# Two gated attention and feed-forward layers in one kernel: all phases in one block, routing by quarters inside the first attention, and expert rows in fixed regions

## The chip, the cores and the metric

One core of a Trainium2 chip runs the whole program. The metric is the device time of one execution in microseconds (us); lower is better.

## What is computed

`x` is 32 batches of 128 rows of 128 numbers, in float32. Four sublayers are added to it one after the other, each on the row-normalised `x`, each scaled by the tanh of a gate. Cut to what matters:

```python
# first attention: one head, 77 keys and values per batch from ctx
Q = ln(x) @ Wq + bq;  K = ctx @ Wk + bk;  V = ctx @ Wv + bv
context = softmax(where(mask == 0, -inf, Q @ K.T / sqrt(128))) @ V
x = x + tanh(g_xattn[0]) * (ln(context) * gamma + beta)
# first feed-forward: 8 experts, one per row, and a shared one
idx = argmax(ln(x) @ router.T)
y = (silu(ln(x) @ gate[idx].T) * (ln(x) @ up[idx].T)) @ down[idx].T
ys = silu(ln(x) @ w_gate_s.T) * (ln(x) @ w_up_s.T) @ w_down_s.T
x = x + tanh(g_ffn[0]) * (y + ys)
# second attention: 16 heads of 8, a bias by distance, padding, projection Wo
x = x + tanh(g_xattn[1]) * (attend(ln(x), ctx) @ Wo + bo)
# second feed-forward: 8 maps of 128 x 128, one chosen per row by signature
x = x + tanh(g_ffn[1]) * (ln(x) @ W[t] + b[t]),  t = argmax(ln(x) @ sign(sigs).T)
```

## The kernel before

Every engine has its program written out by hand; engines meet through semaphores. A block is a set of five programs, one per engine, and ends in a barrier of all engines. There are three blocks.

**Setup** (`build`, L282 to L370). SyncE loads `x` in four quarters of 8 batches into `X`. ScalarE issues 18 small loads (`early`); one semaphore counts them all, so everything that needs any of them waits for the last, `cst`. VectorE computes mean and variance of the rows of `x`, GpSimd the inverse root (`pow`). TensorE multiplies the query and key weights of first attention into one matrix `wqk`. Then SyncE copies the bias table into the tensor `wide_qk` (2048 rows of 77) and issues 10 further loads (`late`).

**First attention** (`attend_0`). Work goes by pairs of batches: 16 pairs, numbered 0 to 15. `pipeline` (L105) gives each engine a list of stages with lags; in a turn an engine runs each stage of its list once, for the pair that stands `lag` pairs back. The middle turns are a loop with registers for the pair's number. Per pair: ScalarE normalises x (`norm`, L555, with `nb0` and `rstd0`); TensorE transposes it and projects the context (`project`, L457 to L463: values of both attentions, `M`, keys of second attention, a row `crow`); ScalarE copies `M` and the keys out (L533); `scores` adds `crow` by a matmul of one row; VectorE adds the mask and takes the maximum `nmax` (`masked`, L589); ScalarE exponentiates; TensorE transposes and multiplies by the values into bank U (`weigh`, L488); VectorE takes the statistics of U (`attend_stats`, L608 to L614) and writes `t1` (L618), with which bank U is free again; GpSimd inverts (`inv_std0`); VectorE writes the new x (`residual`, L628) and its statistics; GpSimd makes `r1` and `nb1` (`inv_std1`, L664 to L670, `pow` in L666); ScalarE normalises (`norm1`, L564), GpSimd copies that into `XN` (L674), TensorE transposes it, ScalarE copies it twice (`xn1T` and `XNT`), and TensorE makes the router's logits, which ScalarE stores in `LG` (L548). SyncE loads context, mask and 1/16 of the expert weights per turn, then fills `sorted_x` with blank rows. At the end VectorE scales the weights `wds`, `wdn`, `wo1`, `bo1`, `w2` and `b2` by the gates (L648).

**Third block**: `feed_forward_0`, then `attend_1`, on each engine one behind the other.

- *Routing.* VectorE takes the argmax for all 32 batches at once (L918 to L923). TensorE counts ranks within and across batches (L807, L808), and VectorE makes from them the row in `sorted_x` where each row of x goes: the rows sorted by expert, each expert's part padded to 128 (L927 to L943), and the table `tile_experts` (L946 to L956), which holds the expert of each of the 39 tiles of 128 rows.
- *Scatters.* GpSimd waits for `slot` and issues 32 indirect DMAs, one per batch, from `XN` to `sorted_x` (L775). Column 128 of each row holds where the result shall go.
- *Shared feed-forward* meanwhile, 6 chunks of 4 batches (`hidden`, L792 and L793; silu, L872; product, L910; `down`, L801; addition, L915). The last two chunks' worth is done in second attention.
- *Expert tiles.* SyncE loads tile after tile from `sorted_x` once all scatters have landed (L769), up to four tiles ahead. TensorE transposes, multiplies by `wgu` of the tile's expert (L832; the expert comes from a register load, L824, one per four tiles), ScalarE and VectorE make `hid`, TensorE multiplies by `wdn` (L848), and GpSimd scatters the result to `routed` (L781).
- *Second attention and feed-forward* go by single batches in a pipeline of 25 stages on TensorE. They are not rewritten.

## Time and profile before

| what | us |
|---|---|
| median of 3 runs (616.97 to 621.12) | 618.58 |
| the profiled execution, its own time | 621.03 |
| its span, from the first to the last instruction | 619.2 |
| TensorE busy | 534.1 (86%) |
| VectorE busy | 403.0 (65%) |
| GpSimd busy | 367.2 (59%) |
| ScalarE busy | 343.9 (56%) |

The shares are means over stages with different limits. TensorE's clock has two levels, 1.2 and 2.4 GHz; the granted clock is given as a share of 2.4 GHz. Engines are named PE (TensorE matmul), PEld (its weight load), DVE (VectorE), ACT (ScalarE), POOL (GpSimd) and SP (SyncE); `q` behind a name is that engine's sequencer. L is the line of the kernel before.

### The profile page before, as it was taken

How to read it: one execution, taken by the hardware profiler on the slowest of the kernel's cores; microseconds unless marked ns; L12 is line 12 of the kernel's file. 1: busy time of each engine (PE TensorE's matmuls, PEld its weight loads, DVE VectorE, ACT ScalarE, POOL GpSimd, SP SyncE). 2: the span in 40 equal slices, each digit the busy share in tenths (PEclk: the TensorE clock that was granted, in tenths of full speed). 3: DMA queues.
4: the chain of work that ended last, by engine and by line, in shares of the span. 5: the costliest groups of instructions: out<-in, count | busy, mean ns of one | idle time of the engine just before them, and what ended most of it. 6: DMA issues, size and time to landing. Idle time of an engine off the chain costs nothing.

```text
span 619.2 us, 14247 instructions
## 1 busy us (share of the span) xinstructions
PE 534.1 (86%) x3643; PEld 339.4 (55%) x3643; DVE 403.0 (65%) x1188; ACT 343.9 (56%) x1013; POOL 367.2 (59%) x740
## 2 busy tenths in 40 slices
PE   0189999769626999989999999999999999999963
PEld 0167777536314666666665565656656566565520
DVE  6138888756103434435888888888888888888731
ACT  0137888531002555528767767677676766767510
POOL 4206677626760555543477776777768777776541
PEclk9989999769677999988999999999999999999965
DMA  7822225401111222210000000000000000000000
GB/s 191 128 78 70 76 74 168 103 1 39 52 51 27 78 76 79 63 35 5 10 11 19 10 17 17 8 17 8 17 15 10 17 8 17 11 10 10 10 5 8
DMA packets 39731, 25.50 MB, mean 41 GB/s; under 512 B 9727, under 2 KB 37025, under 8 KB 39698
## 3 DMA queue, kind: packets, MB, share of 16 engines
q1 hardware_dynamic: 34946, 19.58, 12.4%
q0 software_dynamic: 2272, 4.67, 2.4%
q10 hardware_dynamic: 2480, 0.85, 0.6%
q8 instruction: 15, 0.25, 0.2%
q14 instruction: 18, 0.15, 0.1%
HBM read 15.68 MB, written 10.04 MB: 42 GB/s over the span
## 4 chain that ended last, share of the span: by engine, by line
PE 61%; issue 5%; POOL 4%; another core or an unknown queue 3%; DVE 3%; ACT 1%; DMA 1%; POOLq 0%; SPq 0%; DVEq 0%; ACTq 0%
PE bank L1164 12%; PE bank L1112 10%; PE bank L1103 7%; PE bank L1125 7%; PE bank L1099 3%; POOL routed L781 3%; PE bank L832 3%; PE bank L1136 2%; PE bank L1173 2%; PE bank L792 2%; PE bank L793 2%; PE bank L801 1%; PE bank L1152 1%; PE bank L848 1%
## 5 line engine op out<-in xcount | busy, mean ns | idle before, releaser
L1215 ACT ACTIVATE PRT<-bank 77x512 f32<-77x512 f32 x128 | 74.6, 583 | 18.0 <-PE bank L1112 16.0
L1112 PE MATMUL bank<-cst,SC 128*77 128x128 f32 x512 | 81.0, 281 | 0.2 <-ACT SC L1207 0.2
L1164 PE MATMUL bank<-w,xn3T 128*128 128x512 f32 x128 | 75.7, 675 | 2.5 <-DVE XN L1372 2.0
L1207 ACT ACTIVATE SC<-SC,low 128x77 f32<-128x77 f32 x256 | 67.4, 346 | 1.2
L1112 PEld LDWEIGHTS bank<-cst,SC 128*77 128x77 f32 x512 | 59.6, 150 | 14.5 <-issue 13.9
L781 POOL DMA_INDIRECT routed<-ys,to x39 | 37.2, 953 | 45.4 <-issue 25.4
L1304 DVE TENSOR_TENSOR SC<-bank,biasQ 128x616 f32<-128x616 f32 x64 | 51.1, 799 | 15.3 <-PE bank L1103 15.3
L1125 PE MATMUL bank<-PRT,VP 77*32 77x128 f32 x1024 | 54.5, 285 | 0.7 <-ACT PRT L1215 0.7
L1372 DVE TENSOR_TENSOR XN<-bank,OH 128x512 f32<-128x512 f32 x64 | 44.3, 692 | 15.1 <-PE bank L1164 11.8
L1103 PE MATMUL bank<-KB,QT 32*128 32x308 f32 x256 | 51.6, 480 | 0.0
L1311 DVE TENSOR_REDUCE top<-SC 128x8 f32<-128x616 f32 x64 | 50.5, 789 | 1.1
L1438 POOL TENSOR_TENSOR sum<-XN 128x512 f32<-128x512 f32 x32 | 41.2, 1289 | 15.9 <-DVE XN L1372 15.9
L775 POOL DMA_INDIRECT sorted_x<-XN,slot x32 | 30.9, 965 | 24.2 <-DVE slot L943 14.7
L972 DVE TENSOR_TENSOR hid<-actg,bank 128x256 f32<-128x256 f32 x39 | 16.4, 422 | 39.2 <-ACT actg L882 34.7
L832 PE MATMUL bank<-wgu,xsT 128*128 x78 | 40.9, 606 | 0.3 <-ACT xsT L877 0.3
L1417 POOL TENSOR_TENSOR x2b<-x,bo 128x128 f32<-128x128 f32 x32 | 14.5, 453 | 39.9 <-DVE x L1346 39.9
L1440 POOL TENSOR_TENSOR sum<-sum 128x256 f32<-128x256 f32 x32 | 35.7, 1115 | 2.5
L872 ACT ACTIVATE sg<-bank 128x512 f32<-128x512 f32 x12 | 7.1, 597 | 49.9 <-remote 29.6
L1325 DVE TENSOR_TENSOR SC<-SC,top 128x616 f32<-128x616 f32 x32 | 33.8, 1058 | 0.0
L1125 PEld LDWEIGHTS bank<-PRT,VP 77*32 77x32 f32 x1024 | 20.2, 108 | 24.5 <-issue 18.4
L1243 ACT ACTIVATE xn3T<-bank 128x128 f32<-128x128 f32 x32 | 8.9, 277 | 37.5 <-PE bank L1152 37.5
L1164 PEld LDWEIGHTS bank<-w,xn3T 128*128 128x128 f32 x128 | 19.7, 194 | 18.1 <-ACT OHT L1248 6.9
(222 smaller groups left out, 1295.7 us busy)
## 6 DMA issues: line engine op xcount, KB each, us to landing
sorted_x<-blank SPq DMA_DIRECT2D x10, 258.0 KB, 4.0
xs<-sorted_x SPq DMA_DIRECT2D x39, 64.5 KB
X<-in_x SPq DMA_DIRECT2D x4, 512.0 KB, 7.6
wgu<-in_wgu SPq DMA_DIRECT2D x16, 128.0 KB
y<-routed SPq DMA_DIRECT2D x32, 64.0 KB, 1.8
out<-res SPq DMA_DIRECT2D x32, 64.0 KB, 1.6
ctxT<-in_ctxT SPq DMA_DIRECT2D x16, 77.0 KB, 1.9
mask<-in_mask SPq DMA_DIRECT2D x16, 77.0 KB, 1.9
```

Of the source, the lines that this page charges most:

```text
L781: nc.gpsimd.indirect_dma_start(routed, bass.IndirectOffsetOnAxis(ap=to[:, t:t + 1], axis=0), ys[t % WAYS][:, :], None).then_inc(st_y[t % W ...
L832: nc.tensor.matmul(bH[t % 2][:, :], xsT[t % 2][:, :], wgu[:, bass.ds(experts[t], 1), :], start=True, stop=True).then_inc(e["h"], 1)
L1103: nc.tensor.matmul(bS[i][:, 0:HG * SK], QT[u][rows, :], KB[u][rows, :, :], start=False, stop=True).then_inc(s["sc"], 1)
L1112: last = nc.tensor.transpose(bP[c % 2][0:SK, j * 128:j * 128 + 128], SC[u][:, c * HG + j, :], ident)
L1125: last = nc.tensor.matmul(bO[32 * j:32 * j + 32, c * 128:c * 128 + 128], VP[u][:, c * HG + j, :], PT[c % 2][:, j * 128:j * 128 + 128], sta ...
L1164: nc.tensor.matmul(bF[:, :], xn3T[u][:, :], w2[:, k * HT:(k + 1) * HT, :], start=True, stop=True).then_inc(s["f"], 1)
L1207: last = nc.scalar.activation(SC[u][:, head, :], SC[u][:, head, :], ACT.Exp, bias=low[u][:, head:head + 1])
L1215: nc.scalar.activation(PT[c % 2][:, :], bP[c % 2][0:SK, :], ACT.Copy if c * HG < HH else ACT.Exp).then_inc(s["pTs"], 1)
L1304: nc.vector.tensor_tensor(half(SC[u][:, k, :]), bSS, half(biasQ[:, k, :]), ALU.add).then_inc(s["sb"], 1)
L1311: nc.vector.tensor_reduce(top[u][:, k], SC[u][:, k, :], AX.X, ALU.max).then_inc(s["mx"], 1)
L1372: nc.vector.tensor_tensor(picked[u][:, k * HT:(k + 1) * HT, :], bF[:, :].rearrange("p (t d) -> p t d", t=HT), OH[u][:, k * HT:(k + 1) * HT ...
L1438: nc.gpsimd.tensor_tensor(sum4[u][:, :, :], picked[u][:, 0:4, :], picked[u][:, 4:8, :], ALU.add).then_inc(s["s4"], 1)
```

## The change

**One block.** `everything` builds the parts and runs, on each engine, first attention, feed-forward and second attention one behind the other, with no barrier between setup and the end. First attention is written out for all 16 pairs (`written_out`), with no loop.

**Setup.** ScalarE issues 5 loads in place of 18 (the small ones are packed on the host), each with a semaphore of its own. `x` comes in pieces of 2, 6, 12 and 12 batches, between the loads of the first three pairs. The last 12 loads (`late`: the packed `wc`, the padding, spare rows, expert weights, `w2`, `b2`) go out one per pair.

**First attention.** Scores come from the raw x: the query weights are centred, and the inverse deviation `rstd0` multiplies the scores where the mask is added (`masked`). The normalised copy of x and its transposed form are gone. Mask, key term and constant are summed in one bank by three matmuls (`keys`, with `uqB`, `c0row`, `identb`). The normalised `z` of bank U is now made by ScalarE (`normed`), and bank U is free only then; VectorE multiplies it by the gain and adds `xb`. `norm1` writes `XN` itself, and `XNT` is the one transposed copy. The bias of second attention's values is folded into `bo1`.

**Routing.** When a quarter of 8 batches has its logits, VectorE finds its experts (`route`), a running sum carries the counts over, TensorE ranks (`ranked`), and `slots` gives the rows. Each expert has a fixed region of 4224 rows in `sorted_x`, so that a slot doesn't depend on later counts. The rest of the last 128 rows of a region is filled by 8 loads from a tensor of spare rows (`fill_rows`), and the tiles' rows come from a table by a register load per tile (`tile_rows`). The blank fill of `sorted_x` is gone.

**Scatters.** GpSimd issues all 32 when its part of first attention is over; each waits for its quarter's slots.

**Gates.** VectorE scales `wds`, `wdn`, `wo1`, `w2` in the feed-forward stage. In second attention two tiles, `SC` and `sum4`, lie where `wgu` was, and some semaphores are merged.

```diff
+def written_out(n, stages):
+    first = min(lag for _, lag in stages)
+    for turn in range(n + max(lag for _, lag in stages) - first):
+        for stage, lag in stages:
+            item = turn - (lag - first)
+            if 0 <= item < n:
+                stage(item)
...
+    with nc.Block() as block:
+        @block.gpsimd
+        def _(pool):
+            h["pool_program"](pool)
+            f["pool_program"](pool, h["scatter"])
+            g["pool_program"](pool)
...
+        rows(0)
+        load(0)
+        rows(1)
+        load(1)
+        rows(2)
+        load(2)
+        rows(3)
+        sp.dma_start(m["wide_qk"], bass.AP(tensor=a["table"].tensor, offset=128,
...
+        for g in range(3, NG):
+            load(g)
+            if g - 3 < n_late:
+                sp.dma_start(*late[g - 3]).then_inc(s_late, 16)
...
-            pipeline(pe, NG, [
-                (project, 1), (norm_T, 0), (logits, 6), (probs_T, 2), (norm1_T, 5), (scores, 1), (weigh, 2)])
+        written_out(NG, [(norm1_T, 7), (rows_T, 1), (values, 3), (weigh, 4), (keys, 0), (probs_T, 3), (scores, 1), (ranks, 8), (logits, 7)])
...
-            pipeline(act, NG, [
-                (probs_T, 3), (logits, 7), (norm1_T, 6), (norm, 0), (exps, 2), (norm1, 5), (keys, 1),
-                (norm_T, 0)])
+        written_out(NG, [(values_1, 3), (norm1, 6), (probs_T, 3), (keys, 0), (normed, 4), (exps, 2), (rows_T, 0), (norm1_T, 6)])
...
-            pipeline(dve, NG, [
-                (values, 1), (residual, 3), (masked, 1), (attend_stats, 2), (mask_bias, 0)])
+        written_out(NG, [(values_0, 5), (attend_stats, 6), (residual, 7), (route, 10), (masked, 3), (slots, 10), (mask_bias, 0)])
...
-            pipeline(pool, NG, [
-                (keep, 4), (shifted, 0), (inv_std1, 2), (inv_std0, 1)])
+        written_out(NG, [(inv_std0, 0), (shifted, 0), (inv_std1, 1)])
...
+        def weigh(g):
+            pe.wait_ge(s["pTs"], g + 1)
+            pe.wait_ge(s["v0"], g + 1)
+            wait(pe, s["z"], g)
...
+        def normed(g):
+            act.wait_ge(s["inv"], g + 1)
+            wait(act, s["zg"], g - 1)
+            for b in range(PAIR):
+                last = nc.scalar.activation(z[g % 2][:, b, :], U[:, b, 0:D], ACT.Identity, bias=nr[g % 2][:, b:b + 1],
+                                            scale=ru[g % 2][:, b:b + 1])
+            last.then_inc(s["z"], 1)
...
+    def scatter(pool, b):
+        pool.wait_ge(s["slot"], b // QB + 1)
+        nc.gpsimd.indirect_dma_start(sorted_x, bass.IndirectOffsetOnAxis(ap=slot[:, b:b + 1], axis=0),
+                                     XN[:, b, :], None).then_inc(f["s_scat"], 16)
...
     def pool_program(pool):
-        pool.wait_ge(m["s_zero"], 16 * (SLOTS // 512))
-        pool.wait_ge(s_slot, 1)
         for b in range(B):
-            nc.gpsimd.indirect_dma_start(sorted_x, bass.IndirectOffsetOnAxis(ap=slot[:, b:b + 1], axis=0),
-                                         XN[:, b, :], None).then_inc(s_scat, 16)
+            scatter(pool, b)
...
+        sp.wait_ge(s_fill, 1)
+        for k in range(E):
+            row = sp.value_load(fill_rows[0:1, k:k + 1], min_val=0, max_val=E * REGION - 128)
+            sp.dma_start(sorted_x[bass.ds(row, 128), :], a["spare"][k]).then_inc(s_filled, 16)
...
         for t in range(NTILE):
+            row = sp.value_load(tile_rows[0:1, t:t + 1], min_val=0, max_val=E * REGION + (DUMPS - 1) * 128)
             wait(sp, e["xT"], t - WAYS + 1)
             wait(sp, e["to"], t - WAYS + 1)
-            sp.dma_start(xs[t % WAYS][:, :], sorted_x[128 * t:128 * t + 128, :]).then_inc(l_x[t % WAYS], 16)
+            sp.dma_start(xs[t % WAYS][:, :], sorted_x[bass.ds(row, 128), :]).then_inc(l_x[t % WAYS], 16)
```

GpSimd's stream at the end of first attention, before (`nb` is the shift of `norm1`):

```order
L668 TENSOR_TENSOR mr<-mv,r 128x2 [waits a_r1]
L670 TENSOR_TENSOR nb<-zeros,mr 128x2 [waits a_mr]
L674 COPY XN<-xn 128x2x128 [waits a_xn1] x2
L421 UNCONDITIONAL_BRANCH
L699 UNCONDITIONAL_BRANCH [waits barrier_Pool_Activation_PE_DVE_SP_gather]
L775 DMA sorted_x<-XN,slot 5120x129 [waits r_slot,s_zero]
L775 DMA sorted_x<-XN,slot 5120x129 x31
L781 DMA routed<-ys,to 4608x128 [waits e_ys,e_to] x39
```

and now, at the same place:

```order
L769 TENSOR_TENSOR ve<-mv,eps 128x2 [waits a_xn1,a_xmv]
L770 TENSOR_TENSOR nm<-mv,minus 128x2
L772 TENSOR_TENSOR r<-ve,power 128x2 [waits a_iv1]
L774 TENSOR_TENSOR nb<-nm,r 128x2 [waits a_iv1]
L721 DMA sorted_x<-XN,slot 34688x129 [waits a_slot] x32
L843 DMA routed<-ys,to 5632x128 [waits e_ys,e_to] x39
```

The scatters have moved up past two copies and the barrier, and stand right behind the last `nb`.

VectorE's stream behind first attention, before (all 32 batches are routed at once):

```order
L421 UNCONDITIONAL_BRANCH
L714 UNCONDITIONAL_BRANCH [waits barrier_Pool_Activation_PE_DVE_SP_release]
L918 TENSOR_REDUCE best<-LG 128x32
L919 TENSOR_TENSOR cand<-LG,best 128x256 [waits r_step]
L920 TENSOR_TENSOR cand<-cand,cst 128x256 [waits r_step]
L922 TENSOR_REDUCE best<-cand 128x32 [waits r_step]
L923 TENSOR_TENSOR OH<-cand,best 128x256 [waits r_step]
```

and now, within a turn of first attention (`QH` holds the quarter's choices, `upto` the running counts, `sm` the masked scores):

```order
L679 BN_AGGR mv<-st 128x2
L689 TENSOR_REDUCE best<-bank 128x8 [waits a_lg]
L690 TENSOR_TENSOR cand<-bank,best 128x64 [waits a_stat]
L691 TENSOR_TENSOR cand<-cand,cst 128x64 [waits a_stat]
L693 TENSOR_REDUCE best<-cand 128x8 [waits a_stat]
L697 COPY QH<-upto 128x8 [waits a_stat]
L698 TENSOR_TENSOR QH<-cand,best 128x8x8
L700 SCALAR_TENSOR_TENSOR upto<-cst,QH 128x72 [waits a_stat]
L641 SCALAR_TENSOR_TENSOR sm<-bank,rstd,bias 128x77 [waits a_ex,a_rs,a_sc]
```

Routing has moved from behind the barrier to between two stages of a turn, in four parts of a quarter of the size.

## Rows read from the trace of the kernel before

**Rows 1.** Windows: stretch, us, busy (count) PE PEld DVE ACT POOL, PEclk, DMA share, GB/s

```profile
0.00:27.90 27.90, 1.56 (x8) 1.44 (x8) 12.69 (x73) 2.04 (x8) 9.85 (x14) 1.00 0.77 144
27.90:130.60 102.70, 88.43 (x512) 67.36 (x513) 70.86 (x297) 68.30 (x225) 58.60 (x144) 0.91 0.34 95
130.60:142.70 12.10, 11.40 (x37) 6.45 (x38) 8.70 (x22) 3.87 (x6) 0.00 (x0) 0.88 0.00 1
142.70:194.50 51.80, 30.46 (x115) 18.72 (x114) 12.48 (x28) 5.16 (x10) 30.87 (x32) 0.74 0.15 46
194.50:264.00 69.50, 66.87 (x350) 43.50 (x350) 27.11 (x117) 36.35 (x115) 35.97 (x38) 1.00 0.25 70
264.00:619.20 355.20, 335.35 (x2624) 201.94 (x2624) 271.12 (x652) 228.22 (x651) 231.88 (x514) 0.95 0.04 13
```

**Rows 2.** Timeline of setup: start, us, engine, operation, idle before; and time to landing

```profile
16.15 0.20 ACT L308 ACTIVATE tg<-gates 128x4 f32<-128x4 f32 x1 [4.37 <-DMA cst<-in_cst]
...
27.86 0.88 ACT L555 ACTIVATE xn<-X,nb,rstd 128x128 f32<-128x128 f32 x2 [9.67 <-PEq L280]
...
wide_qk<-in_table SPq DMA_DIRECT2D x1, 616.0 KB, 11.5
```

**Rows 3.** Timeline of ScalarE in first attention, pairs 3 and 15

```profile
50.92 0.39 ACT L533 ACTIVATE M<-bank,m 128x154 f32<-128x154 f32 x1 [1.07 <-PE bank L463]
...
110.67 0.39 ACT L533 ACTIVATE M<-bank,m 128x154 f32<-128x154 f32 x1 [0.21 <-PE bank L463]
```

**Rows 4.** Lines by form, 60 to 100 us: busy us, mean ns, idle before

```profile
L666 POOL TENSOR_TENSOR r<-v1e,power 128x2 f32<-128x2 f32 x8 | 5.8, 722 | 0.6
...
L618 DVE SCALAR_TENSOR_TENSOR t<-bank,mv,gain 128x128 f32<-128x128 f32 x17 | 5.2, 347 | 0.3
...
L608 DVE BATCH_NORM_STATS2 st<-bank 128x6 f32<-128x128 f32 x16 | 3.9, 285 | 0.0
...
L555 ACT ACTIVATE xn<-X,nb,rstd 128x128 f32 x10 | 4.3, 485 | 0.0
...
L599 DVE TENSOR_TENSOR V<-bank,bv 77x256 f32<-77x256 f32 x8 | 3.3, 416 | 0.0
```

**Rows 5.** Timeline at the end of first attention, GpSimd and ScalarE

```profile
122.67 2.16 POOL L666 TENSOR_TENSOR r<-v1e,power 128x2 f32<-128x2 f32 x1
...
126.46 0.19 POOL L670 TENSOR_TENSOR nb<-zeros,mr 128x2 f32<-128x2 f32 x1
...
126.69 0.88 ACT L564 ACTIVATE xn<-X,nb,r 128x128 f32<-128x128 f32 x2 [4.94 <-POOL nb L670]
...
130.12 0.18 ACT L548 ACTIVATE LG<-bank 128x16 f32<-128x16 f32 x1 [1.11 <-PE bank L502]
```

**Rows 6.** Timeline and source line (min/median/max ns, first and last start): routing, scatters

```profile
130.62 0.42 DVE L918 TENSOR_REDUCE best<-LG 128x32 f32<-128x256 f32 x1 [4.29 <-PEq L421]
...
142.75 1.20 POOL L775 DMA_INDIRECT sorted_x<-XN,slot  x1 [14.73 <-DVE slot L943]
...
L775 POOL DMA_INDIRECT sorted_x<-XN,slot x32: 954/958/1204, 142.8 to 182.1; - x32
```

**Rows 7.** Timeline of shared feed-forward and first expert tile

```profile
142.49 1.12 PE L792 MATMUL bank<-XNT,wgs 128*128 128x512 f32 x2 [0.69 <-DVE hT L910]
...
147.84 1.13 PE L792 MATMUL bank<-XNT,wgs 128*128 128x512 f32 x2
...
157.72 0.69 DVE L915 TENSOR_TENSOR X<-X,bank 128x512 f32<-128x512 f32 x1 [4.83 <-remote]
...
187.91 0.69 DVE L915 TENSOR_TENSOR X<-X,bank 128x512 f32<-128x512 f32 x1 [19.74 <-remote]
...
194.48 1.34 PE L832 MATMUL bank<-wgu,xsT 128*128 x2 [0.34 <-ACT xsT L877]
```

**Rows 8.** Source lines of tile scatters and of TensorE's register load

```profile
L781 POOL DMA_INDIRECT routed<-ys,to x39: 952/952/959, 200.8 to 264.6; - x39
...
L824 PEldq TENSOR_LOAD <-tile_experts x10: 297/304/495, 190.0 to 252.5; - x10
```

1067 lines of the change are left out of this document (551 added, 516 removed).

## The prediction

> **What bounds the kernel now.** I read the windows by stage first. The span of 619.2 us is a row of stages that hardly overlap: 27.9 us of setup, 102.7 us of first attention, 12.1 us of routing before the first scatter, 51.8 us from the first scatter to the first expert tile, 69.5 us of expert tiles and 355.2 us of second attention [rows 1]. The change rewrites the first four, 194.5 us; the last two, 424.7 us, keep their instructions but for addresses and semaphores. Then I read the timeline at the seams. ScalarE's first computation waits for `cst`, the last of 18 small loads, until 16.15; first attention starts at 27.86, after 9.67 us behind the barrier [rows 2]. In first attention ScalarE makes the tile `M` of pair 3 (two batches are a pair, 16 in all, counted from 0) at 50.92 and of pair 15 at 110.67 [rows 3]: (110.67-50.92)/12 = 4.98 us a pair. No engine is saturated there: VectorE is busy for 70.9 and ScalarE for 68.3 of 102.7 us [rows 1]. The last pair leaves its router logits at 130.12+0.18 = 130.30; on the way ScalarE waits 4.94 us for GpSimd, whose `pow` took 2.16 us, against 0.72 in the middle of the stage [rows 4, 5]; VectorE was just scaling `wdn`. Routing starts at 130.62, the first scatter at 142.75, the last at 182.11, so they end at 183.07, one per 1.26 us [rows 6].
>
> One thing there is nobody's plan. While the scatters run, the shared feed-forward crawls: VectorE's addition at 157.72 comes after 4.83 us of idling and the next at 187.91 after 19.74, and the first expert matmul comes at 194.48, 11.4 us after the last scatter [rows 7]. The trace doesn't name the cause (it says "remote"); what it shows is that TensorE's results come late, at a mean clock of 0.74 of 2.4 GHz [rows 1], and that it ends 4.8 us after the last scatter.
>
> **The change, part by part.**
>
> *Setup.* Gone are the barrier, 13 of 18 small loads, the wait for all of x and the normalised copy of x. The order of loads is now 2 batches of x, then 6, 12 and 12. What comes late instead is the mask of pair 3: its load stands on SyncE's queue behind all 2.1 MB of x, three pairs' contexts and masks, and the 2048 rows of `wide_qk`; and VectorE, in order, has it ahead of everything of its next turn. With ScalarE's loads that is some 4.1 MB. Before, x and ScalarE's loads, 2.9 MB, were in by 16.15, and `wide_qk` alone took 11.5 us to land [rows 2]. Bounds for pair 3: 14, if the queues share well, and 27.6 (16.15+11.5). The rate of 0.2 MB per us gives 22 (4.1/0.2 and 1.5 to start); as the first loads of x go in larger pieces, I take 20, against 50.92: 30.9 us earlier. Pairs 0 to 2 have their front half done by then.
>
> *Period.* VectorE is busy 70.9/16 = 4.4 us a pair. Out go the two `t` operations (0.35 each) and two of the same form and size for the residual; in come two of 256 columns (0.41 each, by the row of `V`), one small one in the mask (0.19 to 0.35) and a quarter's routing, 9 small ones at 0.2 per 4 pairs, 0.45 a pair [rows 4]: +0.1 net. ScalarE gives up two normalisations (0.49 each) and one of two XNT copies and takes `z` (two of that same form) and V1: no more than before. TensorE adds about 0.35 us and has room. Longer lags take away waits. I take 4.8 us; bounds 4.4 (VectorE's busy time) and 5.5. One loop grows: bank U is now held until ScalarE has made `z`: VectorE's statistics (4 of them, 1.0), GpSimd's four small operations and a `pow` (3 x 0.19 in a row, 0.72 and their waits: 1.6) and `z` (0.9) [rows 4, 5], with the matmuls 4 us if nobody queues; below 4.8, but not by much.
> Pair 15: 20+12x4.8 = 77.6. Before, the drain from there took 130.30-110.67 = 19.6, of which 4.9 was the wait for GpSimd; that goes, as the scaling moved to the feed-forward stage. Of the other 14.7 I make 17, for one more turn of lag and the longer chain. Last logits: 94.6.
>
> *Routing and scatters.* Three of four quarters are routed inside the attention, and GpSimd's stream has the 32 scatters right behind its last `nb`, with no barrier. That `nb` ended at 126.65, 3.65 us before the last logits [rows 5]; at the higher clock I take 2.6, so the first scatter is at 92.0, against 142.75: 50.8 us earlier. Scatters 24 to 31 wait for the last quarter's slots, ready about 4 us after the last logits, at 98.6; scatter 24 is due at 92+24x1.26 = 122.2, so this is covered. Uncovered, every us of it would be a us of the total. End: 92.0+40.3 = 132.3. The scaling of `wdn` and `w2` now lies beside scatters. The `pow` beside it lost 1.4 us and the operation behind it 1.3 (from 122.67 to 126.46, four operations took 3.8 us instead of 1.1) [rows 5]: bounds 0 and 2.7. I take 0.
> The Trainium skill, page "SBUF — State Buffer", section "SBUF: two separate sides", says that a VectorE operation in a two-port mode locks GpSimd out of their shared ports, and that the descriptors of GpSimd's DMAs wait too. By it the scatters would end up to 2.7 us later; the trace agrees for `pow` and has no scatter beside such an operation.
>
> *Fills, table and tile loads.* The 8 fills and their register loads are on SyncE under the scatters. Each of 39 tile loads gets a register load; on TensorE one takes 0.30 us [rows 8], and with its arithmetic and the issue I take 0.8 us of SyncE per tile. The tile period is (264.6-200.8)/38 = 1.68 [rows 8], and loads run up to four tiles ahead. Cost 0, and 0.5 before the first tile, inside the next term. With that cover gone it would be 0.5x39 = 20.
>
> *To the first tile.* The shared feed-forward starts when the last quarter is ranked, at about 97.5, and needs 6 chunks of 5.3 us (142.49 and 147.84 are two starts of the same matmul [rows 7]) and some 4 us: done at 133.5 if nothing disturbs it. The tiles would then follow the scatters by 5.5 us (landing, first load, transposition). Before it was 11.4. As I don't know what the crawl hangs on, I keep 11.4: first tile at 143.7, against 194.5. Bounds: 5.5 and 22 (rival 1).
>
> Sum: 143.7+424.7 = a span of 568.4. The profiled execution took 621.03, 1.8 more than its span, and the median of the runs shown is 618.58, 2.4 below it; so 568.4+1.8-2.4 = **568** us.
>
> **Rivals.**
> 1. *The crawl starts 10 us after the first scatter, as before, whatever the feed-forward has done by then.* Before, it had 2.5 chunks left then, and the crawl let two through. Now it would have over 5 left, and come out 4.8 us after the last scatter with 3.2 to do, 17 us: first tile 62 us after the first scatter, at 154: 578 us. For it: the crawl ends with the scatters. Against it: 8 scatters ran beside full speed.
> 2. *No crawl, and a short period:* 4.5 us, last logits at 91, scatters from 88.4, first tile 5.5 us behind them at 134.2: 558 us. For it: no stage before or after crawls beside indirect DMAs, the tiles' included.
> 3. *The U loop binds a little:* 5.5 us a pair, 12x0.7 = 8.4 more: 576 us. For it: three in-order engines, each over half busy, share the loop.
> 4. *Slower than before, by the same loop:* if VectorE, GpSimd and ScalarE each reach their part only a whole turn after the last one, a pair costs all three turns, about 4.4+3.7+4.3 = 12.4 us: 12x7.6 = 91 more, 659 us. It decides from 4.8+51/12 = 9 us a pair on. For it: the places are fixed by hand. Against it: the lags put the parts of one `z` in neighbouring turns.
>
> **How the numbers follow.** Forecast 0.42, rival 1 0.2, rival 2 0.18, rival 3 0.15, rival 4 0.02, and 0.03 for an unseen wait that eats most of the gain. The forecast's own terms give 8 us either way: pair 3 within 5, the period within 0.3 (x12), the drain within 3, hardly all at once. Reaching out to rivals 1 to 3, the range is 554 to 585. A measurement of this kernel tells about 1%, 6 us, from no change; to come there, 45 us of the gain must be lost. So faster 0.96, same 0.01, slower 0.03.
>
> **What would show it.** `M` of pair 3 near 20 and of pair 15 near 78; 4.8 us between two `nmax`; the first scatter near 92, 2 to 3 us before the last logits; 1.26 us per scatter throughout, with a gap at the 25th only if the last slots are late; the first expert matmul near 144; then 69.5 and 355 us as before. The forecast is wrong if pair 3 waits for something else than its mask, if ScalarE's wait before `z` is over 1 us a pair, if TensorE waits for tile loads, or if the tiles start over 15 us behind the last scatter.

## The result and the profile after

The changed kernel took 599.65 us (median of 4 runs, 598.82 to 602.53), the kernel before 617.78 beside it; the ratio is 0.971, 95% interval 0.9654 to 0.9766. So it is faster, by 18 us. The forecast was 568 (554 to 585). The sign was right; well over half of the forecast gain is missing.

In this and the next fences L is the line of the kernel named. First the windows of the changed kernel's profiled execution, by stage (columns as in [rows 1]): start, first attention from pair 3's keys on, scatters, expert tiles, second attention.

```profile
0.00:29.50 29.50, 17.94 (x71) 13.24 (x72) 14.87 (x77) 6.55 (x24) 4.92 (x13) 0.94 0.98 192
29.50:125.00 95.50, 74.37 (x446) 59.88 (x446) 62.35 (x275) 62.08 (x195) 62.80 (x165) 0.84 0.22 62
125.00:169.50 44.50, 36.04 (x155) 22.68 (x155) 23.58 (x59) 7.72 (x14) 30.16 (x30) 0.88 0.22 62
169.50:240.00 70.50, 69.03 (x343) 43.02 (x343) 26.86 (x115) 36.73 (x115) 34.46 (x36) 0.97 0.25 69
240.00:597.50 357.50, 334.29 (x2634) 201.75 (x2632) 270.95 (x654) 228.89 (x652) 232.77 (x515) 0.96 0.05 13
```

The span is 597.5 (the execution took 599.44). The first expert tile starts 25.0 us earlier than in [rows 7], and 3.3 us are given back behind it: 428.0 instead of 424.7. Now the same points of the program that the forecast named, from the timeline; `M` of pairs 3, 11, 12 and 15 (compare [rows 3]), the last logits, the first scatter, the first tile:

```profile
29.50 0.38 ACT L523 ACTIVATE M<-bank,m 128x154 f32<-128x154 f32 x1
...
67.24 0.38 ACT L523 ACTIVATE M<-bank,m 128x154 f32<-128x154 f32 x1
...
76.36 0.38 ACT L523 ACTIVATE M<-bank,m 128x154 f32<-128x154 f32 x1
...
89.75 0.38 ACT L523 ACTIVATE M<-bank,m 128x154 f32<-128x154 f32 x1
...
121.98 1.20 POOL L721 DMA_INDIRECT sorted_x<-XN,slot  x1 [0.18 <-issue]
...
123.93 1.02 PE L492 MATMUL bank<-wb,XNT 128*128 128x8 f32 x4 [0.47 <-ACT XNT L563]
...
169.49 2.01 PE L900 MATMUL bank<-wgu,xsT 128*128 x2
```

| point | forecast | measured | off by |
|---|---|---|---|
| `M` of pair 3 | 20 | 29.50 | +9.5 |
| `M` of pair 15 | 77.6 | 89.75 | +12.2 |
| last logits end | 94.6 | 124.95 | +30.4 |
| first scatter | 92.0 | 121.98 | +30.0 |
| last scatter ends | 132.3 | 164.0 | +31.7 |
| first expert matmul | 143.7 | 169.49 | +25.8 |
| span | 568.4 | 597.5 | +29.1 |

The turn itself came out shorter than forecast: the `M`s of pairs 7 to 11 stand 4.48 us apart. But between pairs 11 and 12 lie 9.12 us, and from pair 15 on the drain takes 35.2 us instead of 17. These are the two places to look at. A smaller one lies between pairs 5 and 6, whose `M`s are 6.83 us apart; in every other kernel that follows one turn takes 6.4 to 7.3 there too (between pairs 4 and 5 where the lags are one less). GpSimd makes the inverse deviations of the last 12 batches there in one operation, within the loop of the pairs, and the scaling of `norm1` behind it comes late: ScalarE waits 2.72 us for it before 42.96.

```profile
38.33 2.27 POOL L736 TENSOR_TENSOR rstd<-var,power 128x12 f32<-128x12 f32 x1
```

**The long turn.** TensorE and VectorE around the end of quarter 0. `upto` is the last operation of `route`; TensorE's L480 is `ranked`, L429 the values, L468 `weigh`:

```profile
67.85 0.19 DVE L689 TENSOR_REDUCE best<-bank 128x8 f32<-128x64 f32 x1
...
69.52 0.31 DVE L700 TENSOR_TENSOR_SCAN upto<-cst,QH 128x72 f32<-128x72 f32 x1
...
69.88 0.43 PE L480 MATMUL bank<-upto,ones 128*128 128x64 f32 x2 [2.56 <-DVE upto L700]
...
71.59 1.91 PE L429 MATMUL bank<-wb,ctxT 128*77 128x256 f32 x4
...
73.54 0.42 DVE L625 TENSOR_TENSOR V<-bank,rows 77x256 f32<-77x256 f32 x1 [2.08 <-PE bank L429]
```

TensorE reaches `ranked` right behind its `scores`, while VectorE, in order, gets to `route` only behind `residual`. TensorE stands for 2.56 us. Then comes what the wait alone doesn't show: the values take 1.91 us instead of 1.03. The windows around it say why (the column behind the five engines is the granted clock):

```profile
64.00:70.00 6.00, 3.43 (x23) 2.54 (x22) 4.99 (x23) 4.99 (x17) 4.86 (x15) 1.00 0.13 28
70.00:74.00 4.00, 4.00 (x20) 3.39 (x21) 1.77 (x8) 0.66 (x3) 0.15 (x1) 0.61 0.02 4
74.00:78.00 4.00, 4.00 (x29) 3.29 (x28) 3.18 (x15) 3.06 (x10) 2.44 (x8) 0.96 0.61 141
```

TensorE was busy for 3.43 of 6 us, and for most of the next 4 it was granted 1.2 instead of 2.4 GHz. Together the turn is 4.6 us longer. How long the clock stays down differs from run to run: in e4_scale_on_scalar, whose edit lies behind this stage, the same wait of 2.56 us (at 72.37) was followed by the lower level for most of 14 us, and by two long turns, of 11.14 and 7.08 us.

```profile
72.00:80.00 8.00, 7.63 (x30) 6.40 (x31) 4.35 (x19) 1.81 (x5) 1.91 (x6) 0.54 0.23 50
80.00:88.00 8.00, 8.00 (x40) 7.07 (x39) 3.64 (x16) 4.45 (x15) 3.48 (x11) 0.61 0.22 51
```

The same happens at quarter 1 (2.56 at 92.40) and, inside the drain, at quarter 2:

```profile
116.66 0.69 PE L480 MATMUL bank<-upto,ones 128*128 128x64 f32 x2 [4.92 <-DVE upto L700]
...
117.57 0.97 PE L492 MATMUL bank<-wb,XNT 128*128 128x8 f32 x4
```

**The turn in the drain.** One round of the loop through bank U, at a place where the engines have little else to do:

```profile
101.59 0.68 PE L468 MATMUL bank<-V,hT 77*128 77x129 f32 x4 [1.37 <-DVE V L625]
...
102.31 0.50 DVE L652 BATCH_NORM_STATS2 st<-bank 128x6 f32<-128x128 f32 x2 [0.78 <-PE bank L468]
...
103.23 0.28 POOL L756 TENSOR_TENSOR vr<-es 128x2 f32<-128x2 f32 x1 [0.60 <-DVE mv L658]
...
105.11 0.81 ACT L550 ACTIVATE sg<-bank,nr,ru 128x128 f32<-128x128 f32 x2 [1.30 <-POOL nr L763]
...
106.06 0.68 PE L468 MATMUL bank<-V,hT 77*128 77x129 f32 x4 [1.16 <-ACT sg L550]
```

Each step starts as soon as the one before it is done: product, statistics (0.9), GpSimd's five small operations (1.9), `z` (0.8), next product: 106.06-101.59 = 4.47, the period of the full turns. So a turn costs 4.5 us, however empty, as long as a pair still has to go through bank U. The last product into U (pair 15) starts at 110.54. Behind it TensorE waits for quarter 2's `route` (above), and then the turns are short: the logits of the last pairs start 2.0 to 2.4 us apart.

```profile
110.54 1.20 PE L468 MATMUL bank<-V,hT 77*128 77x129 f32 x4 [2.01 <-ACT sg L550]
...
119.53 1.02 PE L492 MATMUL bank<-wb,XNT 128*128 128x8 f32 x4 [0.47 <-ACT XNT L563]
```

The same two points in the kernel before, the last product into U and the last logits:

```profile
115.67 0.70 PE L488 MATMUL bank<-V,PT 77*128 77x129 f32 x4
...
129.05 1.02 PE L502 MATMUL bank<-router,xn1T 128*128 128x8 f32 x4 [0.75 <-ACT XNT L544]
```

From `M` of pair 15 to the last product into U it was 5.0 us and is 20.8; from there to the end of the last logits it was 14.4 (4.9 of them ScalarE's wait for GpSimd) and is 14.4 again.

**The scatters.** All have 0.95 to 0.96 us but the first and two more:

```profile
136.12 1.54 POOL L721 DMA_INDIRECT sorted_x<-XN,slot  x1 [0.31 <-issue]
...
145.55 2.05 POOL L721 DMA_INDIRECT sorted_x<-XN,slot  x1 [0.30 <-issue]
```

Beside them, on VectorE:

```profile
135.35 1.49 DVE L974 TENSOR_SCALAR wdn<-wdn,tg 128x2048 f32<-128x2048 f32 x1
...
145.19 0.75 DVE L974 TENSOR_SCALAR w<-w,tg 128x1024 f32<-128x1024 f32 x1
...
146.05 1.42 DVE L1026 TENSOR_SCALAR padR<-padRi 1x2464 bf16<-1x2464 uint8 x1
```

Last, the crawl of the shared feed-forward [rows 7] isn't there: its last addition is at 162.14, and the tiles follow the last scatter by 5.5 us, not 11.4.

### The profile page after: what moved, and what is told of

It reads as the page before. It is cut to its first block, busy times and chain, and to the rows that moved or that the text cites. A ratio compares the mean times of both kernels' runs of the same rounds, so it can differ in the third digit from the quotient of the medians.

```text
span 597.5 us, 14141 instructions
## 1 busy us (share of the span) xinstructions
PE 531.7 (89%) x3643; PEld 340.6 (57%) x3643; DVE 398.6 (67%) x1178; ACT 342.0 (57%) x997; POOL 365.1 (61%) x758
## 4 chain that ended last, share of the span: by engine, by line
PE 60%; POOL 7%; issue 4%; DMA 4%; ACT 2%; DVE 2%; SPq 0%; POOLq 0%; DVEq 0%; ACTq 0%
PE bank L1233 12%; PE bank L1181 11%; PE bank L1194 8%; PE bank L1172 7%; POOL sorted_x L721 5%; PE bank L900 4%; PE bank L1168 3%; DMA xs<-sorted_x 3%; PE bank L1205 2%; PE bank L1242 2%; PE bank L916 2%; PE bank L1221 1%; PE bank L1159 1%; PE bank L1214 1%; PE bank L1225 1%
## 5 line engine op out<-in xcount | busy, mean ns | idle before, releaser
L1181 PE MATMUL bank<-cst,wgu 128*77 128x128 f32 x512 | 81.1, 281 | 1.0 <-ACT wgu L1276 1.0
L1181 PEld LDWEIGHTS bank<-cst,wgu 128*77 128x77 f32 x512 | 59.5, 150 | 15.5 <-issue 13.9
L1276 ACT ACTIVATE wgu<-wgu,low 128x77 f32<-128x77 f32 x256 | 67.2, 347 | 0.6
L1373 DVE TENSOR_TENSOR wgu<-bank,biasQ 128x616 f32<-128x616 f32 x64 | 51.1, 799 | 11.8 <-PE bank L1172 11.1
L1441 DVE TENSOR_TENSOR XN<-bank,OH 128x512 f32<-128x512 f32 x64 | 44.3, 692 | 17.1 <-PE bank L1233 11.5
L1194 PE MATMUL bank<-PRT,VP 77*32 77x128 f32 x1024 | 55.1, 284 | 0.5 <-ACT PRT L1284 0.5
L1380 DVE TENSOR_REDUCE top<-wgu 128x8 f32<-128x616 f32 x64 | 50.5, 789 | 1.1
L1507 POOL TENSOR_TENSOR wgu<-XN 128x512 f32<-128x512 f32 x32 | 40.4, 1263 | 15.8 <-DVE XN L1441 15.8
L1486 POOL TENSOR_TENSOR x2b<-x,rows 128x128 f32<-128x128 f32 x32 | 14.5, 453 | 39.7 <-DVE x L1415 39.7
L1509 POOL TENSOR_TENSOR wgu<-wgu 128x256 f32<-128x256 f32 x32 | 35.7, 1116 | 2.5
L1394 DVE TENSOR_TENSOR wgu<-wgu,top 128x616 f32<-128x616 f32 x32 | 33.1, 1034 | 0.0
L1172 PEld LDWEIGHTS bank<-KB,QT 32*128 32x128 f32 x256 | 19.2, 183 | 17.0 <-issue 17.0
```

The source lines that it names most:

```text
L1172: nc.tensor.matmul(bS[i][:, 0:HG * SK], QT[u][rows, :], KB[u][rows, :, :], start=False, stop=True).then_inc(s["sc"], 1)
L1181: last = nc.tensor.transpose(bP[c % 2][0:SK, j * 128:j * 128 + 128], SC[u][:, c * HG + j, :], ident)
L1194: last = nc.tensor.matmul(bO[32 * j:32 * j + 32, c * 128:c * 128 + 128], VP[u][:, c * HG + j, :], PT[c % 2][:, j * 128:j * 128 + 128], sta ...
L1276: last = nc.scalar.activation(SC[u][:, head, :], SC[u][:, head, :], ACT.Exp, bias=low[u][:, head:head + 1])
L1373: nc.vector.tensor_tensor(half(SC[u][:, k, :]), bSS, half(biasQ[:, k, :]), ALU.add).then_inc(s["sb"], 1)
L1380: nc.vector.tensor_reduce(top[u][:, k], SC[u][:, k, :], AX.X, ALU.max).then_inc(s["mx"], 1)
```

## The experiments

All kernels are the changed kernel (or, where said, the one before) with the edit shown. As the kernels of one group ran beside each other on one chip (the expectations call that a session) and groups differ, the table gives the kernel before of the same group too. "8 to sc." is the time from `M` of pair 8 to the first of the scatters at the end, which leaves out how a run started; "gap" is from the end of the last scatter to the first expert matmul.

| kernel | us | before | ratio (95%) | `M` 3 | 8 to sc. | gap |
|---|---|---|---|---|---|---|
| changed kernel | 599.65 | 617.78 | 0.971 (0.965-0.977) | 29.50 | 68.2 | 5.5 |
| e1_route_early | 595.72 | 618.32 | 0.969 (0.959-0.978) | 28.97 | 62.0 | 5.4 |
| e2_short_loop | 601.58 | 618.32 | 0.970 (0.954-0.986) | 29.88 | 68.2 | 5.3 |
| e3_window_late | 595.73 | 618.32 | 0.969 (0.957-0.980) | 26.03 | 70.7 | 5.4 |
| e4_scale_on_scalar | 601.21 | 618.32 | 0.975 (0.966-0.984) | 30.79 | 72.3 | 5.4 |
| e5_lags_less_one | 619.94 | 623.3 | 0.992 (0.988-0.996) | 32.10 | 63.8 | 26.7 |
| e6_busy_drain | 629.95 | 623.3 | 1.006 (1.001-1.012) | 28.82 | 79.1 | 25.9 |
| e7_scatter_inside | 608.95 | 623.3 | 0.980 (0.974-0.986) | 28.36 | 68.3 | 26.6 |
| c6_all | 604.4 | 623.3 | 0.969 (0.964-0.975) | 25.75 | 56.6 | 28.4 |
| e8_after_again | 619.98 | 625.14 | 0.991 (0.988-0.994) | 30.50 | 68.1 | 27.3 |
| c6_again | 603.68 | 625.14 | 0.966 (0.962-0.970) | 26.09 | 55.5 | 28.4 |
| e9_spaced (1 run) | 622.43 | 625.14 | | 28.49 | 69.2 | 5.5 |
| e10_before_again (1 run) | 622.54 | 625.14 | | | | 11.5 |
| c7_scatter_inside | 576.39 | 619.67 | 0.934 (0.928-0.940) | 26.10 | 56.9 | 11.1 |
| c8_small_gap | 588.19 | 619.67 | 0.952 (0.945-0.958) | 27.52 | 55.1 | 5.4 |
| c9_order | 583.59 | 619.67 | 0.946 (0.940-0.952) | 30.11 | 56.6 | 11.2 |
| c10_order_gap | 580.75 | 619.67 | 0.942 (0.936-0.949) | 31.31 | 56.8 | 6.5 |
| e11_after_third | 601.75 | 620.27 | 0.975 (0.963-0.987) | 28.71 | 68.2 | 5.4 |
| c7_again | 580.30 | 620.27 | 0.939 (0.929-0.949) | 28.83 | 56.3 | 11.2 |

The executions of one kernel in a group spread over 0.2 to 2.5%, and the changed kernel itself ran in none of the groups e1 to e4, e5 to c6_all and c7 to c10. The ratios of e1 to e4 (0.969 to 0.975) differ from its 0.971 by less than their intervals, so small edits are judged by the trace. There too runs differ: the start of first attention varies by up to 2.7 us between runs of the same kernel (29.50, 30.50, 28.71; 26.10 and 28.83 for c7), and "8 to sc." is 68.1 to 68.2 in the changed kernel's three profiles, but 72.3 in e4, whose edit lies behind that stretch.

### Routing earlier in the turn

```diff
- written_out(NG, [(values_0, 5), (attend_stats, 6), (residual, 7), (route, 10), (masked, 3), ...
+ written_out(NG, [(values_0, 5), (attend_stats, 6), (route, 10), (residual, 7), (masked, 3), ...
- place = lambda q: (bXT if q < NQ - 1 else bLG)[...]      # rows_T waits for `wh`
+ place = lambda q: (bPT if q < NQ - 1 else bLG)[...]      # probs_T waits for `wh`, ranks for `pTs`
```

> Changed kernel with `route` before `residual` in VectorE's turn, and the ranks of quarters 0 to 2 in the bank of the transposed probabilities, so that TensorE's transposition of x no longer waits for `slots`. Theory A (TensorE blocked at `ranks` behind VectorE's `route` is what costs: `M` came 4.6 us late after quarter 0, the `U` product 5.1 us late after quarter 1, and TensorE waited 4.92 us at quarter 2): route ends 1.8 us earlier and the second wait is gone, each of the three gaps shrinks from some 5 us to about 1, first scatter at 122.0-12 = 110, time 588. Theory B (the gap is the price of the routing work itself, which takes 2 us of VectorE wherever it stands and pushes the stages behind it): each gap loses 1 us at most, first scatter at 119, time 597.

The long turn at quarter 0 fell from 9.12 to 6.07 us, as TensorE's wait fell from 2.56 to 0.59 and the values behind it took 1.03 again; the way from pair 8 to the scatters fell by 6.2 us, the first scatter came at 114.27:

```profile
66.41 0.41 PE L480 MATMUL bank<-upto,ones 128*128 128x64 f32 x2 [0.59 <-DVE upto L701]
...
67.76 1.03 PE L428 MATMUL bank<-wb,ctxT 128*77 128x256 f32 x4
```

The first scatter lies midway between the two theories (110 and 119), the time nearer to B: the wait and its clock are a cost of the place, but the 2 us of routing itself stay (this turn and the next are 2.1 us longer than 4.48). At quarter 2, inside the drain, TensorE still waited 2.95 us (4.92 in the changed kernel).

### The loop through bank U made shorter

```diff
- nc.vector.tensor_scalar(es[u][:, :], U[:, :, D], EPS ** 0.5, None, ALU.mult)
+ then(nc.vector.tensor_scalar(es[u][:, :], U[:, :, D], EPS ** 0.5, None, ALU.mult))
+ nc.vector.tensor_tensor(es[u][:, :], es[u][:, :], es[u][:, :], ALU.mult)
- nc.gpsimd.tensor_tensor(vr[u][:, :], es[u][:, :], es[u][:, :], ALU.mult)
- nc.gpsimd.tensor_tensor(vr[u][:, :], vr[u][:, :], mv[u][:, :, 1], ALU.add)
+ nc.gpsimd.tensor_tensor(vr[u][:, :], es[u][:, :], mv[u][:, :, 1], ALU.add)
```

> Changed kernel with the square of `es` on VectorE instead of GpSimd, so that the chain from `mv` to `nr` on GpSimd has one operation less (0.45 to 0.5 us of 1.85), while VectorE gets one small operation more. Theory A (the loop through bank U, product to statistics to GpSimd to `z`, sets the period of 4.48 us, in the steady part and in the drain): period 4.1, 19 turns by 0.4 = 7 us less, first scatter at 115, time 592. Theory B (engines are full: TensorE and ScalarE 17.5 us busy of 20, 3.9 a turn, and in order; VectorE gets longer): period 4.4 or more, at most 2 us less, time 598 to 600.

The period fell, but only from 4.48 to 4.31, and what that gave was lost again in a long turn of 10.28, which kernels with their edits elsewhere had too (10.73 in e3, 10.21 in e9); "8 to sc." is 68.2 as before. A is right that the loop binds (a shorter loop gives a shorter turn), and wrong in what it is worth: 0.17 us further on something else binds. The changed kernel shows the same limit where hardly a pair has reached bank U: its `M`s of pairs 4 and 5 stand 4.31 us apart (32.87 and 37.18). The last group asks what it is.

### The start

```diff
         rows(3)
-        sp.dma_start(m["wide_qk"], ...).then_inc(m["s_window"], 16)
         for g in range(3, NG):
...
+        sp.dma_start(m["wide_qk"], ...).then_inc(m["s_window"], 16)
         for dst, src in late[NG - 3:]:
```

> Changed kernel with the load of `wide_qk` moved from behind x to behind the last pair's mask on SyncE. Theory A (the 2048 rows of `wide_qk` hold up the contexts and masks of pairs 2 and 3): `M` of pair 3 at 29.5-4 = 25.5, time 596. Theory B (x itself and SyncE's own issue, which took 5.30 us for the second context, are what holds them): `M` of pair 3 at 28.5 or later, time within 1 us of 599.7. In both the last late loads come later, at no cost.

`M` of pair 3 came at 26.03: theory A. Of the 9.5 us by which the start missed the forecast, `wide_qk` is 3.5 by these two profiles. By all of them it is about 3: `M` of pair 3 stands at 28.36 to 32.10 in the ten with the early load, and at 25.75 to 28.83 in the six with the late one and the same order of stages on TensorE. In the changed kernel it isn't its own mask that pair 3 waits for last. VectorE waits for the masks of pairs 3 and 4, and only behind the second does it make the first values, which ScalarE has ahead of `M` of pair 3:

```profile
25.86 0.24 DVE L615 TENSOR_SCALAR mb<-mask 128x154 bf16<-128x154 int32 x1 [2.86 <-DMA mask<-in_mask]
...
28.35 0.24 DVE L615 TENSOR_SCALAR mb<-mask 128x154 bf16<-128x154 int32 x1 [1.49 <-DMA mask<-in_mask]
28.50 0.42 DVE L625 TENSOR_TENSOR V<-bank,rows 77x256 f32<-77x256 f32 x1
...
28.95 0.38 ACT L531 ACTIVATE V<-bank 77x256 f32<-77x256 f32 x1 [4.58 <-DVE V L625]
```

In e3 VectorE waits for neither. The masks are late in landing (pair 3's took 9.8 us) and in issue: in the changed kernel the issue of one context beside the loads of x took 5.30 us (it takes 0.45 otherwise), the next two 3.19 and 3.39:

```profile
4.29 5.30 SPq L383 DMA_DIRECT2D ctxT<-in_ctxT  x1
```

The 6 us by which e3 is still late no experiment took apart. In its trace `M` of pair 0 stands at 12.21, and then TensorE is full, with products of nearly double length (the same four for the values take 1.91 and then 1.03 us). The view gives a granted clock of 1.00 for this stretch, so it doesn't explain them:

```profile
13.00:24.00 11.00, 10.79 (x38) 8.70 (x39) 8.72 (x45) 3.55 (x13) 0.15 (x1) 1.00 0.52 152
```

```profile
21.37 1.91 PE L429 MATMUL bank<-wb,ctxT 128*77 128x256 f32 x4
...
26.17 1.03 PE L429 MATMUL bank<-wb,ctxT 128*77 128x256 f32 x4
```

### The scalings beside the scatters

```diff
-        gated(wdn[:, :, :], 2)
-        gated(w2[:, :, :], 3)
-        nc.vector.tensor_scalar(m["padR"]..., m["padRi"][:, :], PADDED, None, ALU.mult)
+    # ScalarE, behind silu of chunks 0, 1 and 2:
+    nc.scalar.activation(wdn[:, :, :], wdn[:, :, :], ACT.Copy, scale=tg[:, 2:3])
+    nc.scalar.activation(w2[:, :, :], w2[:, :, :], ACT.Copy, scale=tg[:, 3:4])
+    nc.scalar.activation(m["padR"]..., m["padRi"][:, :], ACT.Copy, scale=PADDED)
```

> Changed kernel with the scalings of `wdn`, `w2` and `padR` on ScalarE instead of VectorE, beside the same scatters. Theory A (the two scatters of 1.54 and 2.05 us were stretched by VectorE's scalings beside them): all 32 take 0.96 to 1.2, the run of scatters 40.3 instead of 42.0 us, time 598. Theory B (they were stretched by the fills and by traffic): two or more scatters of over 1.4 us remain, time as before within 1 us.

Source line of the scatters, min/median/max ns and first to last start, changed kernel and this one:

```profile
L721 POOL DMA_INDIRECT sorted_x<-XN,slot x32: 954/958/2050, 122.0 to 163.0; - x32
```

```profile
L721 POOL DMA_INDIRECT sorted_x<-XN,slot x32: 954/958/1199, 128.6 to 168.0; - x32
```

Theory A: no scatter is stretched any more, and their run is 40.3 instead of 42.0 us. The fills of `sorted_x` stood beside them in both. The gain of 1.7 us doesn't show in the time, as this profile has `M` of pair 3 at 30.79 and long turns of 11.14 and 7.08 us. The Trainium skill, page "SBUF — State Buffer", section "SBUF: two separate sides", has the rule (VectorE in a two-port mode locks out GpSimd and its descriptors). The trace agrees in that the two stretched scatters stood beside VectorE's scalings and that e4 has none; it doesn't show VectorE's mode, and as e4 moved three scalings at once, it doesn't tell `w2` and `padR` apart for the second. The price is 0.6 and 1.1 us, not the 2.7 I had as the outer bound.

### A turn less of lag, and a busy TensorE

```diff
- PE  (norm1_T, 7), (rows_T, 1), (values, 3), (weigh, 4), (keys, 0), (probs_T, 3), (scores, 1), (ranks, 8), (logits, 7)
+ PE  (norm1_T, 6), (rows_T, 1), (values, 2), (weigh, 3), (keys, 0), (probs_T, 2), (scores, 1), (ranks, 7), (logits, 6)
- ACT (values_1, 3), (norm1, 6), (probs_T, 3), (keys, 0), (normed, 4), (exps, 2), (rows_T, 0), (norm1_T, 6)
+ ACT (values_1, 2), (norm1, 5), (probs_T, 2), (keys, 0), (normed, 3), (exps, 1), (rows_T, 0), (norm1_T, 5)
```

and on VectorE `values_0`, `attend_stats`, `residual`, `route` and `slots` one less each.

> Changed kernel with every lag behind `scores` smaller by one turn on TensorE, ScalarE and VectorE. Theory A (in the drain a turn costs the full 4.48 us of the loop through bank U, whatever little work is in it, so a turn less is 4.5 us less, and the turn was spare, as `exps` used scores that were a turn old): period 4.5 as before, from `M` of pair 15 to the first scatter 27.7 instead of 32.2 us, time 595. Theory B (the turn is needed: without it each engine meets an input that is just being made): period 4.8 or more, which takes back 12 by 0.3 us and more, time 599 or above.

The period stayed 4.48, the long turn of quarter 0 is 9.12 as in the changed kernel, and from pair 8 to the scatters it took 63.8 instead of 68.2 us: the 4.4 us of one turn. The turn taken out lies ahead of bank U. (The long turn of quarter 1 now falls before pair 15's keys, so the drain from pair 15 can't be compared.) Theory A for this stretch. That the time was 620 has another cause, below.

```diff
+        def fill():
+            pe.wait_ge(s["mk"], NG)
+            for _ in range(4):
+                nc.tensor.matmul(bMK[:, 0:2 * D], ident, wv01, start=True, stop=True)
```

> Changed kernel with extra matmuls of 256 columns without use, 4 behind each `logits` and 8 behind each `weigh` from pair 15's keys on, in a bank that is free. They add work and leave none out. Theory A (TensorE's clock is at 0.5 from 110 to 130 us because it idles in the drain, and the operations on the chain to the last logits take twice as long there): clock 0.9 to 1.0 over 100 to 130 us, from `M` of pair 15 to the first scatter 29.5 to 30.5 instead of 32.2 us, time 597. Theory B (the extra matmuls stand ahead of the next turn's work and cost more than the clock gives back, or the clock stays at 0.5): 32 us or more.

Theory B. The clock did stay at 1.00 over 100 to 120 us, where the changed kernel had 0.71, but the extra matmuls made TensorE busy for 20.0 of these 20 us, and from `M` of pair 15 to the first scatter it took 38.7 instead of 32.2 us. (Of the 11 us more in "8 to sc." the other 4.5 lie ahead of pair 15's keys, where the edit adds nothing: turns of 10.99 and 7.23 us with the clock at 0.50 from 70 to 80 us, as in e4.) This tells nothing on what the clock alone costs in the drain: the dose was too large.

### Scatters inside the attention, and all edits together

```diff
+        def scattered(g):
+            for b in range(g, min(g + 1, 8)):
+                scatter(pool, b)
-        written_out(NG, [(inv_std0, 0), (shifted, 0), (inv_std1, 1)])
+        written_out(NG, [(inv_std0, 0), (shifted, 0), (inv_std1, 1), (scattered, 8)])
```

> Changed kernel with the first 8 scatters (quarter 0) issued by GpSimd one per turn in its turns 8 to 15, the other 24 at the end as before. Theory A (GpSimd is busy for 3.4 us of a turn of 4.48, a scatter adds 1.26, so a turn gets 0.2 longer at most; 8 scatters less stand at the end): period of the last turns 4.7, first scatter of the end about 1.5 us later, the run of scatters 10 us shorter, and as the shared feed-forward, done at 162.1 before, becomes what is waited for, first expert tile at 165, time 595. Theory B (the scatter stands in the loop through bank U, which has no slack: each costs its 1.26 us in a turn, and the drain starts 10 us later): first scatter of the end at 132, the feed-forward is done at 172, first expert tile at 174, time 604.

> Changed kernel with the five edits together: route before residual with the ranks in another bank, `es` squared on VectorE, `wide_qk` late, scalings on ScalarE, lags smaller by one. Theory A (they take away waits in different places): first scatter at 122.0-7.7-1.5-3-4.5 = 105.3, the run of scatters 40.3, time 599.7-18.4 = 581. Theory B (a wait taken away in the turn uncovers the next one, as the shorter loop gave only 0.17 us a turn): half of it, 590.

c6_all had its first scatter at 107.53, 14.5 us earlier than the changed kernel, with 40.3 us for the run: theory A up to there. But none of the four kernels of this group was as fast as its front half says. All crawled behind it, with a gap of 26 to 28 us, though the changed kernel had 5.5. This comes next.

### The crawl

> The changed kernel without any edit, beside the others of this group. The last four kernels all crawled between the scatters and the first expert tile (25.9 to 28.4 us from the last scatter's end to the first expert matmul), the first four and the changed kernel not (5.3 to 5.5), though their programs hardly differ there. Theory A (the crawl belongs to the chip or the placement of one session, not to the program): within this group all kernels have it or none; with it the changed kernel takes 620, without it 600. Theory B (it belongs to the program): gap 5.5 us and 600 here, while a kernel such as c6_again crawls beside it.

> The kernel with the five edits together once more. It had its first scatter at 107.53 and the last one's end at 147.86, 16.1 us ahead of the changed kernel's 163.96, and lost 22.9 in the crawl. Theory A (the crawl belongs to the session): without the crawl the first expert matmul comes at 153.5 and the time is 584; with it 604. The difference to the changed kernel beside it is 14 to 16 us in the first case, and in the second also, if the crawl costs both the same. Theory B (it belongs to the program, as its scatters come early against the feed-forward): gap of 28 us here, whatever the changed kernel does.

> The kernel before without any edit. Theory A (crawl of the session): it crawls if the changed kernel beside it does, with 11.4 us from the last scatter to the first expert matmul as in its first profile; if the changed kernel does not, it does not either, and the gap is 5 to 6 us. Theory B (of the program): it crawls, whatever the changed kernel does.

The changed kernel, unedited, now took 619.98 us, with a gap of 27.3, and c6_again 603.68, with 28.4; all kernels of this group with back-to-back scatters crawled, as all of the group before had. In a later group the changed kernel took 601.75 again, with 5.4. So for it the crawl comes and goes with the session, not with the program. Every group of experiments ran on another chip (e1 to e4 on 15, e5 to c6_all on 0, e8 to e10 on 10, c7 to c10 on 5, the last on 9): two chips showed it and three didn't, and chip and session can't be told apart. In a session with it the change gains only 1% (ratio 0.9907). TensorE during it, in e8_after_again, and then SyncE's 8 fills, from the issue of the first to the end of the last, in the changed kernel and in e8:

```profile
149.60 0.37 PE L865 MATMUL bank<-wc,hT 128*128 128x128 f32 x1 [2.64 <-issue]
152.40 0.37 PE L865 MATMUL bank<-wc,hT 128*128 128x128 f32 x1 [2.43 <-issue]
```

```profile
130.45 10.52 SPq L825 DMA_DIRECT2D sorted_x<-in_spare  x8
```

```profile
132.92 38.27 SPq L825 DMA_DIRECT2D sorted_x<-in_spare  x8
```

One matmul in 2.8 us, each behind an idle time that the trace calls "issue": it shows nothing that TensorE waits for. SyncE's fills are slowed as well, to one per 4.8 us instead of 1.3, while a single issue takes 0.70 instead of 0.53 us (medians). What holds the two engines between their instructions isn't shown. Is it the density of the scatters?

```diff
         for b in range(B):
             scatter(pool, b)
+            wait(pool, s_spare, b)
+            nc.gpsimd.memset(m["spare_time"][:, :], 0.0).then_inc(s_spare, 1)    # 700 elements
```

> Changed kernel with a useless memset of about 0.65 us on GpSimd behind each of the 32 scatters, so that they come every 1.9 to 2.0 us instead of every 1.26. It adds work and leaves none out. Theory A (TensorE and SyncE crawl because GpSimd's scatters come back to back and hold up the other engines' instructions or issues): TensorE's crawl is gone or the shared feed-forward runs at least twice as fast beside the scatters as in the kernels that crawl; gap after the last scatter 5 to 6 us. Theory B (the crawl hangs on something that is there as long as scatters are there at all): the crawl is as long as the run of scatters, now 62 us, gap again 25 us. If nothing of this group crawls, this run tells only the price of the spacing, 21 us.

It ran in the same session as e8 and c6_again, which crawled. In it the scatters come every 1.8 to 1.9 us:

```profile
124.39 0.96 POOL L722 DMA_INDIRECT sorted_x<-XN,slot  x1 [0.17 <-issue]
125.35 0.70 POOL L842 MEMSET spare_time<- 128x700 f32 x1
126.21 0.97 POOL L722 DMA_INDIRECT sorted_x<-XN,slot  x1 [0.16 <-issue]
```

```profile
131.04 10.06 SPq L827 DMA_DIRECT2D sorted_x<-in_spare  x8
```

No crawl: the fills are issued in 10.1 us, TensorE is busy for 10.0 of the 10 us from 152 to 162 (1.49 in e8), and the gap is 5.5. Theory A, by one execution. So in these runs the crawl came only with both, a session of that kind and scatters back to back. What differs between sessions isn't shown, nor whether the kernel before crawled in the sessions where the changed one didn't: its page [rows 7] shows the crawl and so does e10_before_again, with a gap of 11.5, but it was not profiled beside a kernel known to be free of it. Its medians were 617.78 to 620.27 us in the sessions without and 623.30 and 625.14 in those with it.

### The last group and the best version

```diff
- PE  ... (weigh, 3), (keys, 0), (probs_T, 2), (scores, 1), ...
+ PE  ... (weigh, 3), (probs_T, 2), (keys, 0), (scores, 1), ...      (c9_order, c10_order_gap)
```

> The kernel with the five edits, and quarter 0's 8 scatters issued one per turn inside first attention. In a session with the crawl the changed kernel gained 11 to 12 us by that move alone (608.95 against 619.98). Theory A (what counts with the crawl is when the scatters end, as TensorE finishes the shared feed-forward only then): again 8 by 1.26 us less, minus 0.5 us for each of 8 turns: 597 with the crawl against 604 of the five edits. Without the crawl the feed-forward is what the tiles wait for: last logits at 108.5, feed-forward done at 108.5+37, first expert matmul at 149, 579. Theory B (in the shorter turns of the five edits GpSimd has no room left, and each scatter costs its 1.26 us in the turn): no gain, 604 with the crawl.

> The kernel with the five edits, and behind each of the 32 scatters a useless memset of 250 elements, 0.2 to 0.3 us, so that they come every 1.5 us instead of 1.26 (a gap of 0.65 us removed the crawl from the changed kernel). Theory A (it takes only a little free time between the scatters for the other engines to go on): no crawl, scatters end 8 to 10 us later, gap 5.5 us, first expert matmul at 105.5+40.3+9+5.5 = 160.5 against 174.3, time 590. Theory B (the gap must be a larger share of the time): still a crawl, first expert matmul at 174 or later, 604 to 612.

> As c7_scatter_inside, and TensorE's `probs_T` ahead of `keys` in its turn. With the five edits the period was 4.31 us and neither the loop through bank U nor ScalarE alone (3.9 busy) explains it. Theory A (a second loop sets it: ScalarE's `z`, TensorE's `weigh`, `keys`, `probs_T`, ScalarE's copy of the probabilities, `M`, `K1T` and `bias`, and `z` again; the new order takes the 1.5 us of `keys` out of it): period 4.0 to 4.1, ten turns by 0.25, first scatter of the end 2 to 3 us earlier than in c7_scatter_inside. Theory B (all engines are near their busy time, about 4.0 on TensorE and 3.9 on ScalarE, and the new order only moves the wait, as `M` now comes later): period 4.3 to 4.5, no gain or a loss.

> As c9_order, with the memset of 0.2 to 0.3 us behind each of the 24 scatters of the end. Theory A (the crawl goes, and with 24 scatters the feed-forward becomes what is waited for): gap after the last scatter about 5 to 10 us, first expert matmul at 152, time 582 in any session. Theory B (the small gap doesn't remove the crawl): 6 us more than c9_order.

This group had no crawl, so the small gap (a scatter every 1.46 us) couldn't show whether it would stop one; without need it cost 5.9 us of scatter run in c8. c7 gave 576.39, the first expert matmul at 149.41 as worked out (149): scatters end at 138.4, and the shared feed-forward is what the tiles wait for. That scatters inside first attention pay is shown in a session with the crawl: beside e5, which crawled like it, e7 took 11.0 us less. In a session without it no kernel ran beside c7 that differs by this alone; c8, with all 32 at the end and the small gaps, took 11.8 us more, of which the gaps are 5.9. Apart from the turns with routing, a turn with a scatter was 4.7 to 4.9 us long in c7 and 4.9 to 5.2 in e7, 0.4 to 0.7 us more than without and not 1.26.

c9's period is 4.27 and 4.40 in turn, not 4.1, and from pair 8 to the scatters it is as long as c7: theory B. It came out 7.2 us slower, 4.0 of them by its start, and at least part of that is the edit's own cost: TensorE now waits 1.76 us for the probabilities of pair 0 (at 21.53) with pair 2's keys behind that, so `M` of pair 2 stands at 24.87 in c9 and in c10, and at 22.08 to 23.70 in the five profiles with the other order. A second loop is thus not shown; in c6_all TensorE was busy for 19.59 of the 20 us from 40 to 60, and that full engines set the last 4.3 us is the likelier reading, not a proven one. c10 took 2.8 us less than c9, about the spread of either, so this doesn't tell whether its gaps cost or gain.

> The changed kernel without any edit, a third time, beside the fastest version found. Theory A (the crawl is a matter of the session): one of its two times, 600 with a gap of 5.5 us from the last scatter to the first expert matmul, or 620 with 27, and the kernel beside it is in the same state. Theory B (it varies from kernel to kernel within a session): the two differ.

> The five edits with 8 scatters inside first attention, again, beside the changed kernel. If the session has no crawl: 576 and 23 to 24 us less than the changed kernel. If it has: scatters of the end from 107 to 138.4, crawl until 143, then the rest of the feed-forward, first expert matmul at 166 to 168, 594, and 25 us less than the changed kernel's 620. Rival: in either, less than 18 us between the two.

Side by side the changed kernel took 601.75 and c7_again 580.30: 21.5 us less, a little below the 23 expected. So the five edits with 8 scatters inside beat both kernels, at a ratio of 0.934 and 0.939 to the kernel before in two sessions, against 0.971 and 0.975 of the changed kernel.

## Why the prediction was wrong

By its own terms:

- *Setup, pair 3 at 20.* Measured 29.50, outside my upper bound of 27.6. Of the 9.5 us, about 3 are `wide_qk` (e3). I summed bytes and divided by a rate; the rate itself was about right, but the small loads came late one after the other, behind single issues of 5.30 and 3.19 us, and what pair 3 waited for last was the mask of pair 4, not its own. Some 6 us are left when VectorE waits for no mask any more; there TensorE is busy for 10.79 of 11 us. I had given TensorE no time in this term. The term was mis-sized.
- *Period, 4.8.* The full turns took 4.48, and the loop through bank U is that period, as the trace of the drain shows and e2 bears out; I had it at 4 us and thought it hidden. Rival 3 named the loop, but with 5.5 us. "No engine is saturated" left out the fullest one: TensorE was busy for 88.4 of the 102.7 us [rows 1], and it is the likely next limit, at 4.3.
- *What the period left out.* Between pairs 5 and 6 GpSimd's one `pow` for 12 batches (2.27 us) makes a turn of 6.83, and the next one took 5.31: 3.2 us. And three times `ranks` stands TensorE behind `route`. I counted the 9 small operations of routing as 0.45 us of VectorE per pair, and not that TensorE would wait for them in its own order and come back at the lower clock. The rule that I had to apply (name what is queued behind a waiting instruction) I applied to the mask and to the scatters, not here. It cost 4.6 us before pair 15 and about 5 in the drain for quarter 1; e1 got 6.2 of it all back. With both, the mean from pair 3 to 15 is 5.02 us a pair, against 4.98 before.
- *Drain, 17.* This is the step that failed most: 35.2. I wrote "one more turn of lag". By the lists, `logits` stands 7 turns behind `keys` now and stood 5 behind `project` before (lags 6 and 1), so even the count was one short. But the turns are not alike. The product into bank U (`weigh`) stands 4 turns behind `keys` and stood 1: three more turns, each at the loop's full 4.5 us. Behind the last product into U there is one turn less, and these are cheap. Of the 20.5 us by which the drain is longer than the 14.7 of before, 15.8 lie ahead of the last product into U (20.8 instead of 5.0 us): `M` of pair 15 stands 2.6 us behind pair 11's product now, and four turns follow, of 9.6 (quarter 1's long one), 4.9, 4.5 and 4.5 us; before, it stood 2.5 ahead of pair 14's product, and one emptied turn of 2.5 followed. The other 4.9 lie behind the last product (14.4 us, and 9.5 before without the wait for GpSimd): TensorE waits 4.92 us for quarter 2's `route`, `residual` of pair 15 waits 2.8 for the same routing on VectorE, and the clock is at 0.50 from 110 to 130 us. These three overlap, and no experiment parts them. e5 measured what a turn of lag ahead of bank U costs: 4.4 us.
- *First scatter 2.6 before the last logits, slots covered.* Right: 3.0, and no gap at the 25th scatter.
- *Scalings beside scatters, 0.* Wrong by 1.7 us, inside the bounds; e4 shows the cause. (Between 122.67 and 126.46 stand two of GpSimd's operations, not four; the 3.8 instead of 1.1 us is right.)
- *Gap of 11.4 to the first tile.* It was 5.5, my lower bound, as the crawl of [rows 7] was absent when it was measured. In sessions with it the gap is 27, and the first tile comes 68 us after the first scatter: rival 1 gave 62 from the same mechanism, with the crawl 10 us behind the first scatter, where e8 has it after 22. That the crawl could be a property of the session I hadn't considered, and the result depends on it: 600 or 620 us. That it was absent made the forecast's miss smaller, and is luck.
- *Tiles and second attention, 424.7.* 428.0. About 1.6 of it is the lower clock at the start of the tiles (the first two `up` products took 2.01 and 1.91, against 1.34 and 1.02 before). The rest isn't settled. The three profiles of the changed kernel have 428.0, 430.0 and 429.6 here, the two of the kernel before 424.7 and 421.8, so some 3 to 8 us are probably the change's own; the edited kernels have 424.0 to 432.2.

The sum of the misses: 9.5 (start) + 2.7 (turns up to pair 15) + 18.2 (drain) - 0.4 + 1.7 (scatters) - 5.9 (gap) + 3.3 = 29.1 us of span.

## What to carry to other kernels

In a pipeline written out by hand, count the turns between the last input and the last output from the lists of before and after, each against its own first stage, and split them at the loop that sets the period: a drained turn ahead of it costs the loop's full length, whatever its work, and one behind it only its own chain. Wherever one engine's stage waits for another's of the same turn, look at what stands ahead of it on that engine: the wait is paid in full, and on TensorE once more at the lower clock. And run a kernel in more than one session, and on more than one chip, before believing a gain of a few per cent, above all if it issues many indirect DMAs back to back.

## What the runs showed of the hardware that was not expected

- In some sessions, beside back-to-back indirect DMAs of GpSimd (one per 1.26 us), TensorE comes down to one matmul per 2.8 us and SyncE to one fill per 4.8 us instead of 1.3; beside one per 1.8 to 1.9 us it doesn't, in the same session (one execution). The effect on the same kernel is 20 us.
- A wait of 2.56 us of TensorE was followed by matmuls at the lower of its two clock levels (1.91 us instead of 1.03 for the same four); a wait of 0.59 us was not. For the same wait the lower level held most of 4 us in one run and most of 14 in another, which cost 4.6 and 9.3 us.
- A VectorE scaling of 1.4 to 1.5 us beside a scatter made that scatter 0.6 to 1.1 us longer; the same work on ScalarE (1.99 us for `wdn`) left all but the first at 0.95 to 0.96.
- SyncE's issue of a small load took 5.30, 3.19 and 3.39 us while large loads were under way, and 0.45 otherwise.
